# Last batch of a graph-attention layer: gate products first, x in a free buffer, the tail taken in two column parts

## The reference

```
h    = x @ W                       # 12 heads of 32 columns
th   = tanh(h);  s = th @ w_src;  d = th @ w_dst      # per head
a    = softmax over neighbours of leaky_relu(s_n + d_m, 0.2)   # masked by adj
z    = a @ h + b ;  e = elu(z)
gate = sigmoid(x @ H_w.T + H_b)
out  = layernorm(x + gate * e + (1 - gate) * x)
```

## Time and profile before

| | us |
|---|---|
| median of 3 runs (lowest, highest) | 736.47 (736.37, 737.73) |
| profiled execution, device time | 738.14 |
| its span, first to last instruction | 736.3 |
| PE busy | 694.9 (94%) |
| DVE busy | 688.7 (94%) |
| ACT busy | 382.0 (52%) |
| POOL busy | 586.6 (80%) |

### The profile page before, as it was taken

How to read it: one execution, slowest core, us unless ns; L and a number is a source line. 1 busy time by engine, 2 the same in 40 slices (tenths; PEclk the granted TensorE clock), 3 DMA queues, 4 the chain that set the end, 5 groups by cost and what they waited for, 6 DMA issues and landing times.

```text
span 736.3 us, 12754 instructions
## 1 busy us (share of the span) xinstructions
PE 694.9 (94%) x3473; PEld 398.2 (54%) x3530; DVE 688.7 (94%) x1283; ACT 382.0 (52%) x807; POOL 586.6 (80%) x434
## 2 busy tenths in 40 slices
PE   8899999999999999999999999999999999999970
PEld 5555556555555655555555555555656555563530
DVE  7899999999999999999999999999999999999876
ACT  5423456373655637365563736556373655636161
POOL 2865897979989797998979799897989989793500
PEclk9999999999999999999999999999999999999995
DMA  5020213111131211113121121213111131111102
GB/s 186 28 74 1 57 44 101 44 44 57 45 100 43 100 43 43 57 43 100 43 100 43 43 57 43 100 43 100 43 43 57 43 100 43 58 44 43 44 1 85
DMA packets 32875, 43.82 MB, mean 60 GB/s; under 512 B 1234, under 2 KB 26580, under 8 KB 32852
## 3 DMA queue, kind: packets, MB, share of 16 engines
q1 hardware_dynamic: 24660, 31.35, 13.8%
q10 hardware_dynamic: 8192, 12.19, 4.6%
HBM read 30.95 MB, written 12.58 MB: 59 GB/s over the span
## 4 chain that ended last, share of the span: by engine, by line
PE 77%; DVE 14%; issue 4%; ACT 2%; DMA 1%; DVEq 0%; POOL 0%; ACTq 0%; SPq 0%; POOLq 0%
PE out_T L879 40%; PE hg L792 26%; DVE ew L638 8%; PE tr L887 4%; PE vb L863 4%; PE hg L848 1%; DVE sd L587 1%; DVE ex L673 1%; ACT h_sb L405 1%; DMA xT_in<-in_xT 1%; DVE att L656 1%; PE hg L853 1%; DVE ex L735 1%; DVE th_w L572 0%; DMA out<-y 0%
## 5 line engine op out<-in xcount | busy, mean ns | idle before, releaser
L638 DVE SCALAR_TENSOR_TENSOR ew<-vb,u,adj_in 128x512 f32<-128x512 f32 x768 | 533.3, 738 | 1.8 <-PE vb L863 1.8
L879 PE MATMUL out_T<-ew,vals 128*64 128x512 f32 x1536 | 361.1, 600 | 2.8 <-DVE ew L638 1.3
L879 PEld LDWEIGHTS out_T<-ew,vals 128*64 128x64 f32 x1536 | 110.3, 136 | 195.2 <-issue 161.9
L274 POOL TENSOR_TENSOR th_w<-th,score_w 128x768 f32<-128x768 f32 x58 | 107.4, 1852 | 64.7 <-ACT th L401 54.5
L434 ACT ACTIVATE att_T<-out_T,tiny 128x512 f32<-128x512 f32 x96 | 66.2, 689 | 140.6 <-PE out_T L879 140.4
L792 PE MATMUL hg<-w_hi,xT_hi 128*128 128x384 f32 x384 | 108.5, 391 | 10.0 <-ACT h_sb L405 6.6
L792 PE MATMUL hg<-w_lo,xT_hi 128*128 128x384 f32 x384 | 88.4, 338 | 0.0
L792 PE MATMUL hg<-w_hi,xT_lo 128*128 128x384 f32 x384 | 88.0, 337 | 0.0
L278 POOL TENSOR_TENSOR th_w<-th_w 128x384 f32<-128x384 f32 x58 | 78.1, 1346 | 4.5
L411 ACT ACTIVATE gate_tanh<-hg 128x384 f32<-128x384 f32 x64 | 31.4, 491 | 96.0 <-PE hg L792 96.0
L792 PEld LDWEIGHTS hg<-w_hi,xT_hi 128*128 128x128 f32 x384 | 69.7, 192 | 19.3 <-issue 15.3
(11 more groups left out here) (107 smaller groups left out, 791.6 us busy)
## 6 DMA issues: line engine op xcount, KB each, us to landing
xT_in<-in_xT SPq DMA_DIRECT2D x16, 768.0 KB, 4.7
x_in<-in_x SPq DMA_DIRECT2D x16, 768.0 KB, 4.5
out<-y ACTq DMA_DIRECT2D x15, 768.0 KB, 3.5
adj_in<-in_adjT SPq DMA_DIRECT2D x16, 256.0 KB, 4.9
ew<-in_W SPq DMA_DIRECT2D x1, 576.0 KB, 4.3
scratch<-in_HwT SPq DMA_DIRECT2D x1, 576.0 KB, 8.0
score_w<-in_w_rows SPq DMA_DIRECT2D x1, 384.0 KB, 7.2
out<-y SPq DMA_DIRECT2D x1, 384.0 KB, 2.5
```

Of the source, the lines that this page charges most:

```text
L274: g.tensor_tensor(th_w[:, c % 2], th[:, c].unsqueeze(1).broadcast_to([P, 2, D]), score_w[:], ALU.mult).then_inc(S["thw_done"], 1)
L638: ve.scalar_tensor_tensor(out=ew[:, (2 * C * j + i) % SLOTS, :], in0=VB[h % 4][:], scalar=u[:, q, c, h:h + 1], in1=adj_in[:, q, c, :], op0 ...
L879: te.matmul(OUT[VW * k:VW * k + VW, :], vals[:, q, c, h, :], ew[:, t % SLOTS, :], start=(c == 0), stop=(c == C - 1)).then_inc(S["ew_free"], 1)
```

## The change

In the last step PE takes the gate product of chunk 0 ahead of attend 0, of chunk 1 behind attend 0, of chunks 2 and 3 behind attend 1, and the mean behind attend 2. ACT follows that order. The last batch's x is loaded into `xT_in`, seen as `x_last`. `y_last` is the tile `ex`, so the last batch doesn't write `y`. ACT makes `x + 1` and `gate` inside the step and copies the mean, times `alone`, into `mean_last` (the tile `th`). POOL makes `rest_last = x - gate * (x + 1)`.

The columns are split at LATE = 256, that is 8 of 12 heads. For the early 256: POOL adds the mean, ACT makes relu(1-att), relu(att-1) and exp of minus the first, POOL adds the last two, which is elu+1; all this stands ahead of the copy of the last pair on ACT. DVE's `after()` begins with the multiplication by `gate` and the addition of `rest_last` for them. Then come the last quotients, the mean for the late 128 columns, eight `bn_stats` of 128 columns, the late elu, multiply and add, four more `bn_stats`, and `bn_aggr` over three groups. `normalise(14)` on ACT stands behind the late Exp. `pow` waits for the variance alone.

The diff, cut to its core and with the indent halved (removed lines stand in the kernel above; in `after()` of DVE everything between the quotients and the wait for `rstd_done` is replaced):

```diff
+stats = sb("stats", [P, C, 3, 6])
...
+x_last = xT_in[:].rearrange("p k n -> p (k n)").rearrange("p (c d) -> p c d", d=D)
+mean_last = th
+rest_last = x_plus1
+above_last = gate_tanh
+y_last = ex
...
+LATE = 4 * VW
...
+    if last:
+      sp.wait_ge(S["xhi_done"], C * B)
+      sp.wait_ge(S["xlo_done"], C * B)
+      sp.dma_start(x_last, x_v[b]).then_inc(S["ld_x_last"], 16)
+      return
...
   def after():
...
+    sp.dma_start(out_v[B - 1][:, 2:C], y_last[:, 2:C]).then_inc(S["st_last"], 16)
...
+    if last:
+      gated_rest()
...
       mean(b - 1)
+    if last:
+      rest()
+      add_means_early(q)
...
       scale(b - 1)
+    if last:
+      elu_early()
   def after():
...
+    pool.wait_ge(S["moments"], C + 1)
+    g.tensor_tensor(rstd[:], var[:], half[:], ALU.pow).then_inc(S["rstd_done"], 1)
+    pool.wait_ge(S["moments"], C + 2)
+    pool.wait_ge(S["rstd_done"], 2 * B - 1)
+    g.tensor_tensor(shift[:], neg_mean[:], rstd[:], ALU.mult).then_inc(S["rstd_done"], 1)
+  def gated_rest():
+    pool.wait_ge(S["gate1_done"], B)
+    pool.wait_ge(S["x_forms_done"], B)
+    g.tensor_tensor(rest_last[:], gate[:], x_plus1[:], ALU.mult).then_inc(S["rest_last_done"], 1)
+  def rest():
+    pool.wait_ge(S["rest_last_done"], 1)
+    g.tensor_tensor(rest_last[:], x_last, rest_last[:], ALU.subtract).then_inc(S["rest_last_done"], 1)
+  def add_means_early(q):
+    pool.wait_ge(S["att_done"], HP * (B - 1) + 4)
+    pool.wait_ge(S["mean_last_done"], C)
+    g.tensor_tensor(att[:, q, :, 0:LATE], att[:, q, :, 0:LATE], mean_last[:, :, 0:LATE],
+            ALU.add).then_inc(S["att_last_done"], 1)
+  def elu_early():
+    pool.wait_ge(S["exp_last_done"], 3)
+    g.tensor_tensor(y_last[:, :, 0:LATE], y_last[:, :, 0:LATE], above_last[:, :, 0:LATE],
+            ALU.add).then_inc(S["elu_last_done"], 1)
...
   def step(b, q, first, last, ahead=True):
+    if last:
+      step_last(b, q)
+      return
...
+  def step_last(b, q):
+    normalise(b - 2)
+    gate_quarter(b - 1)
+    x_forms(b - 1)
+    copy_out(b, 0)
+    gates(b, 0)
+    elu_exp(b - 1, 1 - q)
+    copy_out(b, 1)
+    gates(b, 1)
+    gates(b, 2)
+    copy_out(b, 2)
+    gates(b, 3)
+    x_last_form()
+    gate_quarter(b)
+    row_sums(b - 1)
+    copy_out(b, 3)
+    means_alone()
+    row_squares(b - 1)
+    copy_out(b, 4)
+    exp_early(q)
+    copy_out(b, 5)
+  def x_last_form():
+    act.wait_ge(S["ld_x_last"], 16)
+    act.wait_ge(S["mixed"], 3 * (B - 1) + 1)
+    a.activation(x_plus1[:], x_last, ACT.Identity, bias=plus1[:, 0:1]).then_inc(S["x_forms_done"], 1)
+  def means_alone():
+    act.wait_ge(S["hm_done"], B)
+    act.wait_ge(S["alone_done"], B)
+    for c in range(C):
+      a.activation(mean_last[:, c], mean_ps, ACT.Copy, scale=alone[:, c:c + 1]).then_inc(S["mean_last_done"], 1)
+  def exp_early(q):
+    act.wait_ge(S["att_last_done"], 1)
+    act.wait_ge(S["mixed"], 3 * (B - 1) + 3)
+    a.activation(y_last[:, :, 0:LATE], att[:, q, :, 0:LATE], ACT.Relu, bias=plus1[:, 0:1],
+          scale=-1.0).then_inc(S["exp_last_done"], 1)
+    act.wait_ge(S["gate1_done"], B)
+    a.activation(above_last[:, :, 0:LATE], att[:, q, :, 0:LATE], ACT.Relu,
+          bias=minus1[:, 0:1]).then_inc(S["exp_last_done"], 1)
+    act.wait_ge(S["exp_last_done"], 2)
+    a.activation(y_last[:, :, 0:LATE], y_last[:, :, 0:LATE], ACT.Exp, scale=-1.0).then_inc(S["exp_last_done"], 1)
   def after():
...
+    q = (B - 1) % 2
+    act.wait_ge(S["att_last_done"], 2)
+    a.activation(y_last[:, :, LATE:D], att[:, q, :, LATE:D], ACT.Exp, bias=minus1[:, 0:1]).then_inc(S["exp_last_done"], 1)
     normalise(B - 2)
...
+      a.activation(y_last[:, c], y_last[:, c], ACT.Identity, bias=shift[:, c:c + 1],
...
+    act.dma_start(out_v[B - 1][:, 0:2], y_last[:, 0:2]).then_inc(S["st_y"], 16)
...
   def step(b, q, first, last, ahead=True):
...
   def after():
...
+    early = (slice(None), slice(None), slice(0, LATE))
+    late = (slice(None), slice(None), slice(LATE, D))
+    def statistics(k):
+      for c in range(C):
+        ve.bn_stats(stats[:, c, k], y_last[:, c, P * k:P * (k + 1)]).then_inc(S["stats_done"], 1)
+    dve.wait_ge(S["elu_last_done"], 1)
+    dve.wait_ge(S["rest_last_done"], 2)
+    ve.tensor_tensor(y_last[early], y_last[early], gate[early], ALU.mult).then_inc(S["y_last_done"], 1)
+    dve.wait_ge(S["y_last_done"], 1)
+    ve.tensor_tensor(y_last[early], y_last[early], rest_last[early], ALU.add).then_inc(S["y_last_done"], 1)
     for f in attended(B - 1, q, HP - 1):
       f()
...
+    dve.wait_ge(S["att_done"], HP * B)
+    ve.tensor_tensor(att[:, q, :, LATE:D], att[:, q, :, LATE:D], mean_last[late],
+            ALU.add).then_inc(S["att_last_done"], 1)
+    dve.wait_ge(S["y_last_done"], 2)
+    for k in range(2):
+      statistics(k)
+    dve.wait_ge(S["exp_last_done"], 4)
+    ve.scalar_tensor_tensor(out=y_last[late], in0=y_last[late], scalar=1.0, in1=att[:, q, :, LATE:D], op0=ALU.min,
+                op1=ALU.max).then_inc(S["elu_last_done"], 1)
+    dve.wait_ge(S["elu_last_done"], 2)
+    ve.tensor_tensor(y_last[late], y_last[late], gate[late], ALU.mult).then_inc(S["y_last_done"], 1)
+    dve.wait_ge(S["y_last_done"], 3)
+    ve.tensor_tensor(y_last[late], y_last[late], rest_last[late], ALU.add).then_inc(S["y_last_done"], 1)
+    dve.wait_ge(S["y_last_done"], 4)
+    statistics(2)
+    dve.wait_ge(S["stats_done"], 3 * C)
+    for c in range(C):
+      ve.bn_aggr(mv[:, c], stats[:, c]).then_inc(S["moments"], 1)
+    dve.wait_ge(S["moments"], C)
+    dve.wait_ge(S["y_done"], C * (B - 1))
+    dve.wait_ge(S["rstd_done"], 2 * (B - 1))
+    ve.tensor_scalar(var[:], mv[:, :, 1], EPS / 4, None, ALU.add).then_inc(S["moments"], 1)
+    ve.tensor_scalar(neg_mean[:], mv[:, :, 0], -1.0, None, ALU.mult).then_inc(S["moments"], 1)
...
+      ve.tensor_scalar(y_last[:, c], y_last[:, c], rstd[:, c:c + 1], shift[:, c:c + 1],
...
+  def step_last(b, q):
+    broadcast_v(b, q, 2)
+    transpose_out(b - 1, HP - 1)
+    broadcast_v(b, q, 3)
+    gates(b, q, 0, True)
+    for j in range(HP):
+      attend(b, q, j)
+      if j + 1 == HP:
+        break
+      if j + 2 < HP:
+        broadcast_v(b, q, 2 * j + 4)
+      if j == 0:
+        gates(b, q, 1, True)
+      if j == 1:
+        gates(b, q, 2, True)
+      transpose_out(b, j)
+      if j + 2 < HP:
+        broadcast_v(b, q, 2 * j + 5)
+      if j == 1:
+        gates(b, q, 3, True)
+      if j == 2:
+        means(b, q)
+    if last:
+      step_last(b, q)
+      return
```

More of the change, by code:

```diff
@@ L115, in gat_layernorm @@
         squares = sb("squares", [P, C])
-        stats = sb("stats", [P, C, 6])
+        stats = sb("stats", [P, C, 3, 6])
         mv = sb("mv", [P, C, 2])
@@ L143, in gat_layernorm @@
             vb_ready ew_ready ew_free outT_copied tr_done inv_done att_done
-            alone_done att1_done x_forms_done gate1_done elu_exp_done elu_done mixed moments sums_done mean_done squares_done var_done rstd_done y_done last_mixed last_y_done""".split()
+            alone_done att1_done x_forms_done gate1_done elu_exp_done elu_done mixed moments sums_done mean_done squares_done var_done rstd_done y_done ld_x_last mean_last_done rest_last_done att_last_done exp_last_done elu_last_done y_last_done stats_done last_y_done""".split()
         S = {n: sem(n) for n in names}
@@ L148, in gat_layernorm @@
         NEX = 5
-        NMO = 2 * C + 2
+        LATE = 4 * VW
         def feature_bank(b, c):
@@ L214, in after @@
                 sp.wait_ge(S["last_y_done"], 2)
-                sp.dma_start(out_v[B - 1][:, 2:C], y[:, 2:C]).then_inc(S["st_last"], 16)
+                sp.dma_start(out_v[B - 1][:, 2:C], y_last[:, 2:C]).then_inc(S["st_last"], 16)
                 sp.wait_ge(S["st_y"], 16 * B + 16)
@@ L355, in step @@
                     scale(b - 1)
+                if last:
+                    elu_early()
             def after():
-                pool.wait_ge(S["moments"], NMO)
-                scale(B - 1)
+                pool.wait_ge(S["moments"], C + 1)
[19 more added lines that the diff above has]
+                                ALU.add).then_inc(S["elu_last_done"], 1)
             program(pool, step, before, after)
@@ L510, in after @@
             def after():
-                gate_quarter(B - 1)
-                x_forms(B - 1)
+                q = (B - 1) % 2
+                act.wait_ge(S["att_last_done"], 2)
+                a.activation(y_last[:, :, LATE:D], att[:, q, :, LATE:D], ACT.Exp, bias=minus1[:, 0:1]).then_inc(S["exp_last_done"], 1)
                 normalise(B - 2)
-                act.wait_ge(S["att1_done"], C * B)
-                for c in range(C):
-                    a.activation(ex[:, c], att[:, (B - 1) % 2, c], ACT.Exp, bias=minus1[:, 0:1]).then_inc(S["elu_exp_done"], 1)
@@ L518, in after @@
                 act.wait_ge(S["rstd_done"], 2 * B)
                 for c in range(2):
-                    a.activation(y[:, c], y[:, c], ACT.Identity, bias=shift[:, c:c + 1],
```

(15 more changed lines are left out.)

## The result

The changed kernel took 730.62 us (median of 4 runs, 729.88 to 732.09) against 736.55 us before (4 runs, 736.37 to 737.73): ratio 0.992, 95% interval [0.9902, 0.9938], 5.9 us less. The lowest runs are 6.5 us apart (729.88 and 736.37). Forecast: 730.3 (727.8 to 733.5).

What follows compares the result with a forecast made beforehand. PE and DVE are both busy 94%, so the last batch and its tail were the question: tail start 714.8 plus 15.3 gives a 730.1 us span against 736.3; 6.2 off the median 736.47 gives 730.3 us, range 727.8 to 733.5.

Steps and rivals of the forecast that it cites:

- Last products: Last batch's attend and gate products on PE: the reorder gives 0.5 us by itself, DVE's last edge at 710.3 to 710.5.
- Load of x: Last x into xT_in, issued at 657.5 with 38 us to land: costs nothing; as late as before, 2.7 us.
- Early chain: 256 of 384 columns through ACT and POOL, from gate at 699.05 to elu_early at 714.7; DVE idles 4.2 us.
- T: When DVE's tail starts, behind POOL's elu_early: 714.8.
- Tail: From the start of DVE's tail to the end of the span: 15.3 us, with short statistics stepping by 0.20.
- Sum: 714.8 + 15.3 = 730.1 us of span against 736.3: 6.2 us less, taken from the median 736.47.
- The two rules: Trainium skill: VectorE fixed latency, 0.29 us per short statistic, sum 731.4; DVE and GpSimd port exclusion, nothing stalls in new chain.
- The forecast's "only": Port rule as forecast: only a DVE instruction with two SBUF inputs and a GpSimd one reading SBUF exclude each other.
- DVE starting its tail without a wait: Rival: early chain done by 710.5, so DVE never waits; span 725.8, time 726.0; chance 0.17 (less held or not).
- Order costs: Rival: gate 2's wait, late copies and Relu, Relu, Exp cost more; DVE's tail starts at 717, time 732.5; chance 0.20.
- slower: Rival: GpSimd's four large last-batch operations run 2.4 times longer beside DVE's edges, 16 us more, 746.7; chance 0.04.
- no effect: Rival: early half ends too late for the late third to hide anything; tail starts near 721, 736.5; chance 0.04.

Runs made afterwards that it cites:

- quotients first: The changed kernel with the last quotients and the late mean ahead of the early multiply in DVE's tail: 729.66 us, ratio 0.99 to before.
- longer GpSimd: The changed kernel with one more GpSimd pass of 1536 elements behind gated_rest: 734.26 us, ratio 0.9963 to before.
- more warm-up alone: The changed kernel with only three more warm-up matmuls ahead of the first features: 730.17 us, ratio 0.9912 to before.

## Why the prediction was right

The mechanism held at each step of the walk. Times of after are given with 1.67 us added, to compare with the prediction's scale.

- **Last products.** Attend 1 was held by `elu(14)` and ended at 684.1 + 1.67 = 685.8 (forecast 685.75); gate 2 began at 686.9 (686.9). DVE waited 1.47, 1.47 and 0.15 us (1.5, 1.2, 0.1). Its last edge ended at 710.7, where 710.3 to 710.5 was forecast: the reorder by itself gave DVE 0.1 us, not 0.3 to 0.5, since the second wait was 1.5 and not 1.2.
- **Load of x.** Hidden, as said; undone it cost 3.0 us (2.7 said). The load took 4.5 us from issue to use, where the forecast took the 3.54 of the store.
- **Early chain.** `gate` ended at 699.2 (699.05), GpSimd's passes took 3.47, 3.47, 2.36 and 2.35 us (3.48, 3.48, 2.38, 2.38). T came at 714.4 instead of 714.8, since handing over cost less than I allowed. DVE's idle time was 3.69 us (4.2).
- **Tail.** 15.38 us from T to the end (15.3). The statistics' step was 0.19 us ((1.64 - 0.87) / 4, from eight and four of them). Aggregation 0.52. `shift` ended at 723.21 + 1.67 = 724.9 (725.3).
- **Sum.** 6.53 us in the changed part against 6.2, mostly because T came 0.4 us early. Taken from 736.47 that is 729.9, which two of the four runs have. The other two took 731.3 and 732.1 and put the median at 730.62, so part of its closeness to 730.3 is luck: two misses of opposite sign. That the slower two paid for a low clock is likely and not shown, as neither was profiled. This is the one thing that the prediction left out. It saw the added pause of PE and priced it by what waits behind, but not by what the pause can do to the clock of the work that follows it; that was 1.35 us in three profiled executions.
- **The two rules.** By the formula of the Trainium skill (VectorE: DVE Perf Modes, "The TRN2 errata"), which it gives for an fp32 add, each short statistic is 0.29 us. By the two rows one does last that long (0.87 less three steps), but the next one starts after 0.19; the sum with 0.29 each, 731.4, was too high for this part, and four long ones were 0.26 us slower. The rule of the Trainium skill on shared ports (SBUF — State Buffer, "Who interferes with whom") held: nothing stalled in the new chain, and where an experiment did put two such instructions side by side, one lost 0.22 us. The forecast's "only" was too strong, for that section also names VectorE's two-port modes; no row of the new chain bears on it.
- **Rivals.** DVE starting its tail without a wait came only when the elu was moved to DVE. Order costs, slower, and no effect did not occur; no effect is what the split gives without the order.

## What to carry to other kernels

Work taken ahead of the last products pays only from the moment its last input is known: move the producers of that input first (here the gates) and read the chain from there to the tail. When an engine idles ahead of its tail, give it the slowest link of the chain it is waiting for, even if that adds work to the engine that bounds the rest: one Exp and 1.22 us on DVE in place of 5.7 us over ACT and GpSimd (706.99 to 712.72) gained 2.5 us. Before comparing two profiles, anchor both at the same instruction, the last one that the change doesn't reach.

## What the hardware showed that I had not expected

PE's pause of 0.84 us between matmuls was followed in three profiled executions by a granted clock of 0.50 for about 3 us (three products of a gate 1.16 us instead of 0.68), and in six others by none. PE's program is the same up to there in the three and in the changed kernel, which is one of the six. PE had stood idle for 0.77 to 0.82 us a little before as well, ahead of the last two products of attend 1, in all nine. What decides between the two stays open.

The first warm-up of 12 matmuls took 4.13 us in one execution and 5.30 in another. Where it was short PE paused 2.29 us ahead of the first features and the clock was 0.51 to 0.64 from 7 to 11 us; where it was long the pause was 0.92 us and the clock 1.00. The other profiles fall in line: 4.13 and 4.21 us with pauses of 2.14 and 2.08 and the low clock (quotients first, longer GpSimd), 5.07 to 5.30 us with pauses up to 1.66 and a clock of 1.00 in the eight others with 12 matmuls. With 15 one took 5.36 us, which is the pace of the short kind, and its pause was 1.31 us and its clock 1.00 (more warm-up alone). Why the warm-up itself has two lengths stays open: the profile shows a granted clock of 1.00 through both.
